# Attention stage of a fused adaLN block on eight cores: the output projection of a tile is issued inside the next tile's head loop, and the head pipeline runs two heads deeper

## The reference, cut to what matters

```
mod = (silu(c) @ wmod).reshape(4, 6, 1, -1)      # sa, ca, ga, sb, cb, gb
h = layernorm(x) * (1 + ca) + sa
# inside _L0_attn_ref(h, ...):
q, k, v = layernorm(h) @ qkv_w.T                 # 16 heads of 64
sim  = einsum('bnid,bnjd->bnij', q * 64**-0.5, kk)   # 128 queries x 384 keys
sim  = where(valid, sim, neg)                    # the window before the first and behind the last
attn = softmax(sim)
attn_out = einsum('bnij,bnjd->bnid', attn, vv)
x1 = h + attn_out @ proj_w.T + proj_b
y  = x1 + fc2(gelu(fc1(layernorm(x1))))
x  = x + ga * y
# then: a second adaLN, 8 experts with 2 chosen by softmax gates, and
# x + gb * experts(...)
```

## Time and profile before

| | |
|---|---|
| median of the runs shown | 2973.79 us (2 runs, 2961.46 and 2986.11) |
| the profiled execution | 2966.76 us |
| its span, slowest core (core 4) | 2964.8 us |
| spans of the eight cores | 2948.4 to 2964.8 us, granted clock 0.752 to 0.755 |
| TensorE matmuls busy over the span | 1811.2 us (61%) |
| VectorE, ScalarE busy over the span | 811.0 us (27%), 782.0 us (26%) |
| attention stage on core 4, first score matmul to the first load behind its barrier | 832.0 to 1411.0 us |

### The profile page before, as it was taken

How to read it: one execution, slowest core, us unless ns; L and a number is a source line. 1 busy time by engine, 2 the same in 40 slices (tenths; PEclk the granted TensorE clock), 3 DMA queues, 4 the chain that set the end, 5 groups by cost and what they waited for, 6 DMA issues and landing times.

```text
span 2964.8 us, 32175 instructions; the slowest of 8 cores (2948.4 to 2964.8 us)
## 1 busy us (share of the span) xinstructions
PE 1811.2 (61%) x10437; PEld 934.8 (32%) x10437; DVE 811.0 (27%) x1708; ACT 782.0 (26%) x1694; POOL 70.4 (2%) x132
## 2 busy tenths in 40 slices
PE   0320354545866666667334888888721159999999
PEld 0100121212433333333122555555510024444443
DVE  2214323232123333433223111111123322111112
ACT  0002223222233333343101222222233322222222
POOL 0000000000000000000111000000011100000000
PEclk9855677777955555555666888888855579999999
DMA  8242111111242222220565111110156611110110
GB/s 258 85 128 92 57 54 68 57 50 64 89 125 76 89 86 72 76 93 28 171 192 160 43 43 41 39 43 29 43 178 204 206 57 40 50 36 36 36 36 32
DMA packets 109424, 249.35 MB, mean 84 GB/s; under 512 B 30505, under 2 KB 44977, under 8 KB 107214
## 3 DMA queue, kind: packets, MB, share of 16 engines
q1 hardware_dynamic: 71088, 153.42, 16.9%
q10 hardware_dynamic: 27938, 60.33, 5.2%
q0 software_dynamic: 10240, 33.56, 3.5%
HBM read 186.95 MB, written 60.32 MB: 83 GB/s over the span
## 4 chain that ended last, share of the span: by engine, by line
PE 53%; DVE 17%; DMA 13%; ACT 7%; issue 7%; ACTq 1%; DVEq 1%; SPq 0%; PEldq 0%; POOL 0%; PEld 0%; POOLq 0%
PE bank L1650 7%; PE bank L1204 7%; PE bank L1183 6%; PE bank L1664 6%; PE bank L658 5%; DMA arena<-wfc2T 4%; PE bank L943 3%; PE bank L842 3%; PE bank L899 3%; DMA arena<-wmod 3%; DMA arena<-w_in 2%; PE bank L692 2%; DMA arena<-wqkvT 2%; DVE arena L880 2%; PE bank L867 1%
## 5 line engine op out<-in xcount | busy, mean ns | idle before, releaser
L1204 PE MATMUL bank<-arena 128*128 128x256 bf16 x2048 | 288.1, 289 | 158.3 <-DVE arena L1117 101.3
L1204 PEld LDWEIGHTS bank<-arena 128*128 128x128 bf16 x2048 | 210.5, 103 | 250.2 <-issue 170.1
L1183 PE MATMUL bank<-arena 128*128 128x512 bf16 x1024 | 273.5, 392 | 0.4 <-ACT arena L1212 0.4
L1664 PE MATMUL bank<-arena 128*128 128x512 bf16 x1024 | 244.1, 381 | 3.6 <-DMA arena<-s_h2T 3.6
L628 PE MATMUL bank<-ident_bf,arena 128*128 128x128 bf16 x144 | 18.2, 307 | 362.4 <-DVE arena L622 362.4
L1650 PE MATMUL bank<-arena 128*128 128x512 bf16 x1024 | 239.3, 379 | 0.0
L1212 ACT ACTIVATE arena<-bank,arena 128x256 bf16<-128x256 f32 x256 | 121.2, 474 | 426.6 <-PE bank L1204 426.6
L842 PE MATMUL bank<-ident_bf,arena 128*128 128x128 bf16 x768 | 127.7, 304 | 100.2 <-ACT arena L912 100.1
L1673 ACT ACTIVATE arena<-bank 128x512 f32<-128x512 f32 x128 | 76.4, 597 | 378.0 <-PE bank L1667 264.9
L1677 DVE TENSOR_SCALAR arena<-arena 128x512 bf16<-128x512 f32 x128 | 62.2, 486 | 375.8 <-ACT arena L1673 375.8
L658 PE MATMUL bank<-arena 128*128 128x512 bf16 (+1 forms) x640 | 158.1, 396 | 2.2 <-ACT arena L670 1.1
(11 more groups left out here) (183 smaller groups left out, 2137.7 us busy)
## 6 DMA issues: line engine op xcount, KB each, us to landing
arena<-wmod SPq DMA_DIRECT2D x16, 1536.0 KB, 9.5
arena<-x_ext SPq DMA_DIRECT2D x34, 512.0 KB, 5.2
arena<-wfc2T POOLq DMA_DIRECT2D x64, 256.0 KB, 4.4
arena<-wfc1T SPq DMA_DIRECT2D x64, 256.0 KB, 4.3
arena<-w_in POOLq DMA_DIRECT2D x64, 256.0 KB, 4.4
arena<-s_s SPq DMA_DIRECT2D x32, 512.0 KB, 5.1
arena<-w_in SPq DMA_DIRECT2D x64, 256.0 KB, 5.3
arena<-wqkvT SPq DMA_DIRECT2D x24, 512.0 KB, 4.4
```

Of the source, the lines that this page charges most:

```text
L1183: st=tT_r[mu % 2]: e.matmul(bf(b)[:, :], st[:, l * 128:(l + 1) * 128], wfc2_bf[:, mm * 1024 + nn * 512: mm * 1024 + nn * 512 + 512], start ...
L1204: e.matmul(bf(b)[:, 0:256], wfc1_bf[:, kk * DFF + mm * 128: kk * DFF + mm * 128 + 128], zt[:, kk * 256:(kk + 1) * 256], start=(kk == 0), s ...
L1664: e.matmul(bf(b)[:, :], ht[:, ts(kk, 128)], w1_bf[:, (ee * 8 + kk) * 512:(ee * 8 + kk) * 512 + 512], start=(kk == 0), stop=False))
```

## The change

Three things change, all in the attention stage.

1. The projection and everything behind it move into a function `tail_proj(t)`. It is called for tile t-1 inside the head loop of tile t, behind what is emitted for h == 6, and for the last tile behind the loop. The eight transposes of ao_sb and the copy to aoT_sb stay at the end of their own tile. TensorE's wait for that copy moves into `tail_proj`; the copy itself gets a wait for the previous tile's projection, since aoT_sb has one buffer; and the transposes of odd heads, which share bank 5 with the ao_sb transposes, get a wait for the last copy out of it.
2. In the head loop the transposes run two heads behind the scores (one before) and the values four heads behind (two before). Behind the last head the list has two heads of transposes and then four heads of values.
3. p_sb and pT_sb get four buffers each instead of three, one index changed from `idx % 3` to `idx % 4` wherever they are used.

```
-    p_sb = [A.alloc(f"psb{i}", [128, WIN], BF16) for i in range(3)]
-    pT_sb = [A.alloc(f"pTsb{i}", [128, WIN], BF16) for i in range(3)]
+    p_sb = [A.alloc(f"psb{i}", [128, WIN], BF16) for i in range(4)]
+    pT_sb = [A.alloc(f"pTsb{i}", [128, WIN], BF16) for i in range(4)]
...
+    def tail_proj(t):
+        waitr("tensor", SAOE, t + 1)
+        waitr("tensor", SX1, t)
+        E.wait("tensor", WCAST, wcast_proj)
...
         def emit_tr_copy(idx):
             tb = 2 if idx % 2 == 0 else 5
             waitr("tensor", SEXP, idx + 1)
             waitr("tensor", SPTEp[idx % 2], idx // 2)
+            if tb == 5:
+                waitr("tensor", SAOE, idx // HEADS)
...
-            if h > 0:
-                emit_tr_copy(idx - 1)
-            if h > 1:
-                emit_v(idx - 2)
-        emit_tr_copy(t * HEADS + HEADS - 1)
-        emit_v(t * HEADS + HEADS - 2)
-        emit_v(t * HEADS + HEADS - 1)
+            if h > 1:
+                emit_tr_copy(idx - 2)
+            if h > 3:
+                emit_v(idx - 4)
+            if h == 6 and t > 0:
+                tail_proj(t - 1)
+        for fl in (HEADS - 2, HEADS - 1):
+            emit_tr_copy(t * HEADS + fl)
+        for fl in (HEADS - 4, HEADS - 3, HEADS - 2, HEADS - 1):
+            emit_v(t * HEADS + fl)
...
         E.wait("vector", SAOT, SAOT.n)
+        waitr("vector", SPRJ, t)
         E.op("vector", lambda e: e.tensor_copy(aoT_sb[:, :], bb(5)[:, 0:D]),
              inc=SAOE.bump())
-        E.wait("tensor", SAOE, SAOE.n)
-        waitr("tensor", SX1, t)
...
+    tail_proj(NT_OWN - 1)
```

250 lines of the change are left out of this document (125 added, 125 removed).

## The result

The changed kernel takes 2898.24 us (median of 11 runs, 2893.7 to 3006.23), the kernel before 2960.98 us in the same comparison (10 runs, 2957.85 to 3000.77). The ratio is 0.9762, with a 95% interval of 0.9726 to 0.9799: faster by 2.4%, some 70 us by the ratio (the two medians lie 63 us apart). The forecast was 2921 us, a gain of 46 us, within a range of 2890 to 2952 us. The direction and the range held; "within 2%" was the case that I held likeliest and it did not come, and a quarter to a third of the gain was not in my sum.

A forecast was written before the change was run, and what follows sets the result against it. TensorE was taken to set the heads' pace at 1.2 GHz, with waits idling it between them. Terms of -17.5, -19.2, -20.7 and +11.1 summed to -46.3 us, from 2966.8 to a forecast 2921 us; 8-in-10 range 2890 to 2952 us.

The forecast's parts named there:

- a: Projection's wait for the copy to aoT_sb goes, except the last tile's 1.16 us: -17.5 us.
- b: Behind the projection, two more transposes and values run during the tail: -19.2 us; some 5.8 us wait moves to scores 9.
- c: Stalls within the heads, values waiting for VectorE's copy and short transpose waits, go: -20.7 us.
- d: At a tile's start, scores 2 must wait for the exponential of head 0: +0.44 us.
- e: At a tile's end, four heads of values in a row, and transposes 15 may wait: taken as +0.30 us.
- f: At the restart behind the tail, VectorE's copy of head 5 is queued later: nothing, with a bound of +0.4 us.
- g: The projection itself, 16 + 2 matmuls: left unchanged, with clock-dependent bounds of -8 us and +14 us.
- h: Before the ao_sb transposes, the 2.06 us wait for the last multiplications stays.
- Rival 4: Attention stage gains more, through an earlier clock and cheap seams: -60 us or more, 2905 us or less; chance 0.10.
- Rival 2: Only the seams go; work moved into the tail's shadow returns as refill bubbles: -27 us, 2939 us; chance 0.20.
- Rival 3: Mid-tile restart never regains the stream, heads behind it at 2.4 us each: about 3057 us; chance 0.05.
- Rival 1: Clock stays at 2.4 GHz through heads behind the projection: -28 us more, 2892 us; chance 0.10.

The follow-up runs named there:

- The two gap runs: Changed kernel with two unused VectorE row sums holding TensorE directly ahead of the projection (2957.82 us, ratio 1.0012) or three heads earlier (2942.26 us, ratio 0.993).
- the deferring version: Changed kernel with tail spread over heads, stores on SyncE, projection at head 4, ao_sb transposes behind next tile's head 2: 2789.61 us, ratio 0.9426.
- the kernel with 0.3 us inserted: Changed kernel plus an unused 256-column row sum on VectorE ahead of each tile's second multiplications: 2899.03 us, one execution.

## Why the prediction was right, and where it was not

**a, the copy wait.** One entry of 1.2 us remains, as forecast (1.16).

**b, two heads into the shadow of the tail.** Borne out. The open stretch is 6.69 us against 6.79, two whole heads lie in it, and the wait that moved to scores 9 is 5.36 us where I had said 5.8: I had priced the two heads inside it at 1.0 us, and they take 1.33. The difference costs nothing, since only what left the rest of the tile counts. The run with the tail alone shows the same from the other side: with one head of transposes and values in the shadow instead of two, its wait is 5.91 us on average against 5.32.

**c, the stalls in the heads.** Values no longer appear among the waits, and the 1.00 us wait of the earlier trace rows has no successor.

**d, e, f, the new seams.** d was right. The wait at a tile's start is listed as 0.70 to 0.80 us, not 0.44, but that is because scores 0 and 1, standing directly behind each other, take 0.60 us together and not the 0.86 that I took; scores 2 start 1.31 us behind scores 0 (1167.51 to 1168.82), and the step had said 1.30. e was somewhat too cheap: from scores 15 to the ao_sb transposes it is 5.48 us on average against 4.89 before, and the sum makes it 5.34 (one head of transposes and two of values more, 0.70 us of stalls less, 0.30 for the seam). f was too cheap within its bound: the restart waits 0.19 to 0.28 us (0.54 in some tiles), and the first head behind it takes 1.29 us, 0.26 over the steady 1.03, where I took nothing. Together that is 0.4 us per tile more than the sum. It was given back by a term that I did not have: the heads run at 1.03 us and not 1.07, 0.56 us over fourteen heads. The depth of the pipeline is the cause of this, as the two halves show: 1.03 us with the deeper pipeline alone, 1.02 to 1.15 with the tail alone. Without the projection the mean period fell from 29.33 to 26.10 us, 3.23 us against the 3.1 of the sum. So the sum's total for everything but the clock was right within 2 us over the stage, partly because these errors cancel. About 3 us more came from the first and the last tile.

**g, the projection: the step that was mis-sized.** "The projection itself ... I leave it", with a bound of -8 us. It measured -15.3 us, twice the bound. The step had taken the best tile of the kernel before as the earliest that the clock could rise. But no tile of that kernel has heads directly ahead of the projection; in every one a wait for the copy stands there. Each microsecond by which the clock rises earlier saves half a microsecond of projection: 2.24 us earlier on average makes 1.1, and 1.02 was measured. The two gap runs, which differ only in where the idle stands, show the cause and give the size again (5.84 against 4.83 us). The full size is in part luck: what heads ahead bring for certain is a range of rises that begins at 0.5 instead of 2.1 us, and where in it the tiles fall hangs on the period. The tail alone, with heads ahead too, has a projection shorter by 0.47 us and not by 1.02. With the 15.3 us the sum is 46.3 + 15.3 = 61.6 us, and the stage gave 66.3.

The Trainium skill ("TensorE: Matmul & The Clock Gate", Part 4, PE-mode transpose) has it that a transpose does not count as busy for the clock. For heads by themselves the trace agrees with what I drew from it, 6.03 us of heads without a gap at 0.50. For heads that lead into a projection it does not carry: with them directly ahead the rise comes 1.8 us on average behind the start of the first 512-column matmul, and 4.0 us when a gap stands there. The head is a mix of transposes and short matmuls, and no run here separates their shares. I had used the page's rule against any help by the heads, and the measurement decides: they do not lift the clock themselves, but with them ahead it rises sooner in the projection.

**h** stayed (16 entries, 33.4 us), until the deferring version took it.

**The rivals.** Rival 4, an earlier clock with cheap seams at 2905 us or less, is what happened as far as the clock goes; the seams e and f were not cheap. I gave it 0.10, and the mechanism was in my own bound for g; it should have been a term with both ends far wider. Rival 2 (only the seams go) fell: the shadow brought what it should. Rival 3 (slower, the stream not regained) fell: behind the restart the heads are at 1.03 us with one wait of 0.2. Rival 1 (the clock stays up) did not come in the changed kernel, as I had argued from the idle behind the two heads, 5.4 us, and came for some seven microseconds per tile once the tail was spread. Its price of 0.175 us for a head's scores at 2.4 GHz was misread: the six matmuls in 0.35 us are two heads whose scores overlap (they start 0.08 us apart there), and a lone head's scores hold TensorE for 0.27 us (1178.55 to 1178.82). The signs that I had named held: one entry for the copy, one wait of about 5.5 us at scores, clock 0.50 in the heads. The distance between projections did not: 30.94 us against 32.2.

## What to carry to other kernels

Before counting a wait as only its own length, look at what stands directly behind it: if that is a block of large matmuls, the idle time ahead also sets how long the block runs at the low clock, here 1 us of projection per tile on top of the wait. A tail moved off its place but left in one piece on the in-order list of the engine that feeds TensorE only moves its wait; cut in pieces between the heads, and with its store issues on the queue that only issues transfers, it gave 70 us more than the move itself. And a transform that is two changes in one should be priced in halves: here the halves saved 2.5 us per tile and the whole 4.25.

## What the runs showed of the hardware

- Heads (128-column matmuls, transposes, 64-column matmuls) never left 1.2 GHz by themselves, with TensorE 6.03 of 6.03 us busy: in each of the eleven kernels all 128 rises of the clock in the stage (16 on each of eight cores) lie in the 128 projections. Directly ahead of 512-column matmuls heads brought the rise forward, from 4.0 us on average (2.2 to 6.0) with a gap there to 1.8 (0.5 to 3.5) with the gap three heads earlier.
- The same heads kept 2.4 GHz behind the projection, from 999.39 to 1006.69, at 0.73 busy (3.94 of 5.40 us), when no long idle stood between. So which level such a mix runs at depended on what went before, not only on the mix. But it did not hold for good: the clock fell 6.7 to 8.6 us behind the last bias in 99 of 128 projections, with no idle above 0.94 us before.
- The rise within one kernel varies by three microseconds and more from tile to tile. On core 3 of the kernel with 0.3 us inserted it follows the period: unchanged at 1.36 us while the period is 30.72 us, and sooner by the difference where the period is longer, until it jumps back (1.19 to 4.04 us). The means of kernels with heads up to the projection (1.8, 3.0 and 3.2 us) differ by where their tiles fall in the range.
- Scores of two neighbouring heads, three matmuls of 128 columns with a contraction of 64 rows each, take 0.60 us together at 1.2 GHz and 0.35 at 2.4 GHz when they stand directly behind each other, and start 0.15 and 0.08 us apart on average; separated by other work each holds TensorE for 0.43 us at 1.2 GHz.
- Four heads of values in a row, twelve matmuls of 64 columns, take 1.14 us from the first start to the last end. In the stream a head of values adds less, 0.17 us in the changed kernel (heads take 0.86 us without values at a tile's start and 1.03 with them).
